# Query denominators summed four chunks at a time in eight partitions, in a graph layer fused with linear attention and a gated feed-forward

## The chip, the cores and the metric

The kernel runs on one core of a Trainium2 chip. The metric is device time in microseconds (us), the median of several executions. Beside the median stands one profiled execution, from which all rows below are read; its span runs from the first to the last instruction of the engines.

## The reference

`x` has 1250 rows (nodes) of 1024 columns, in float32. The layer normalises it, adds a graph convolution over 41,250 edges and a linear attention with 16 heads, and adds a gated feed-forward of a second normalisation. What matters here is the attention:

```python
phiQ = elu_plus_one(Q);  phiK = elu_plus_one(K)          # (1, 16, 1250, 64) each
S = jnp.einsum('bhki,bhkj->bhij', phiK, V)
Z = phiK.sum(axis=-2)                                     # one vector of 64 per head
num = jnp.einsum('bhqi,bhij->bhqj', phiQ, S)
denom = jnp.einsum('bhqi,bhi->bhq', phiQ, Z)[..., None] + EPS
context = num / denom
```

The kernel divides `phiQ` by the denominator before the product with `S`. A denominator is one number per head and node, so 16 x 1250 numbers in all.

## The kernel before, in words

Activations lie transposed, features in partitions. Every large product is made of three single-pass products of float32r parts: a value is split into a high part (a copy with rounding, by ScalarE) and a low part (the difference, by VectorE or GpSimd), and high x high, low x high and high x low are summed in PSUM. Weights stream from DRAM in slices of 128 x 512 into a ring of 10 slots, split there by ScalarE (`hi`, line 753) and GpSimd (`weight_lo`, line 443). A slot is free for its next slice when TensorE has used it for the last time, so each slab of weights follows TensorE closely at the switch from one slab to the next.

The stages in order are: keys and values (40 units), queries (24 units, lines 1552 to 1554), the graph's `h` units (20, lines 1431 to 1433), aggregation, mixing with `Wo`, and the feed-forward. The change lies in the query stage and the first `h` units. The queries are 8 blocks of 128 features (two heads each) times 3 chunks of nodes (418, 416, 416). I call the 24 units product 0 to 23, in the order in which TensorE makes them; each has 24 matmuls. Before, the chunk runs fastest. Each engine has its own program in order, joined by semaphores:

- TensorE: product i, then the denominator of i-2 (`denominator`, line 1568). The two slabs switch between products 11 and 12; after product 23 come the `h` units, the first of which has denominator 22 behind it and the second denominator 23.
- VectorE, for each i: `q_min` (line 1196, PSUM to `qmin`), `den_invert(i-3)` (line 1212, the reciprocal), `q_add` (line 1206, writes `phiq`), `den_apply(i-3)` (line 1219, `phiq` times the reciprocal).
- ScalarE, for each i: the exponential (line 832), the relu (line 835, which frees the PSUM bank), `den_copy(i-2)` (line 820, PSUM plus epsilon to `rec`). At i = 11 and 23 it makes six `hi` copies of the next slab before the exponential and two behind it.
- SyncE: `phin_store` (line 472) puts the divided `phiq` into DRAM (`phin_d`), one block of 1250 columns at a time, from three buffers.

Three PSUM banks serve all units in turn. The denominator before is one float32 product per unit: the stationary operand `zblk` is 128 x 128, with the sums of `phik` over the nodes copied along 64 columns for each head, so that each of the 128 partitions gets its head's denominator already in place.

Of the kernel before, what the change touches and what calls it, by code (L numbers as in the profile page):

```python
# [58 lines left out]
PHI_BUFS = 3  # L59
# [50 lines left out]

def units():

    u = [("kv", s, t) for s in range(4) for t in range(NT)]
    u += [("q", 0, 0), ("z", 0), ("z", 1)]
    u += [("q", f, c) for f in range(KD) for c in range(3) if f or c]
# [48 lines left out]
def build(nc, x, src_rows, dst_rows, wslices, wo, bkv, bq, gb, bo, scales, w3s, out):  # L164
    with ExitStack() as ctx:
# [53 lines left out]
        with ExitStack() as r2:  # L219
            hs = sb("hs", [P, 2, NT, 512], F32R, r2)  # L220
# [24 lines left out]
        with ExitStack() as r3:  # L245
            zblk = sb("zblk", [P, KD, P], F32, r3)
            qmin = sb("qmin", [P, 2, 418], F32, r3)
            qrel = sb("qrel", [P, 2, 418], F32, r3)
            rec = sb("rec", [P, 2, 418], F32, r3)
            phiq = sb("phiq", [P, PHI_BUFS, N], F32, r3)  # L250
# [14 lines left out]

        phin_d = nc.dram_tensor("phin_d", [KD, P, N], F32, kind="Internal").ap()
# [55 lines left out]
        den_done = sem("den_done")  # L322
# [130 lines left out]
        def _(sp):  # L453
# [16 lines left out]
            def phin_store(f):  # L470
                sp.wait_ge(phin_ready, 3 * (f + 1))
                sp.dma_start(phin_d[f], phiq[:, f % PHI_BUFS, :]).then_inc(phin_stored[f % PHI_BUFS], 16)
# [18 lines left out]
            for step in range(64):  # L491
# [7 lines left out]
                if step >= 40 and (step - 40) % 3 == 2 and (step - 40) // 3 >= 1:  # L499
                    phin_store((step - 40) // 3 - 1)  # L500
            phin_store(KD - 1)

            for b in range(PHI_BUFS):
                sp.wait_ge(phin_stored[b], 16 * len(range(b, KD, PHI_BUFS)))
# [113 lines left out]
        def _(pool):  # L618
# [65 lines left out]
            for b in range(PHI_BUFS):  # L684
                pool.wait_ge(phin_stored[b], 16 * len(range(b, KD, PHI_BUFS)))
# [21 lines left out]
        def _(act):  # L707
# [93 lines left out]
            def sums_out():  # L801
# [4 lines left out]
                for i in range(2):  # L806
                    u = UNIT["z", i]
                    wait_full(act, u)
                    act.wait_ge(z_cleared, 1)
                    z_ps = PS[:, bank(u), :].rearrange("p (a b) -> p a b", a=4)  # L810
                    nc.scalar.activation(zblk[0:64, 4 * i:4 * i + 4, 0:64], z_ps[0:64, :, 0:64], ACT.Copy)
                    nc.scalar.activation(zblk[64:P, 4 * i:4 * i + 4, 64:P], z_ps[64:P, :, 64:P],
                                         ACT.Copy).then_inc(acc_free[bank(u)], 1)

            def den_copy(i):
                n = CHUNKS[i % 3][1]
                act.wait_ge(den_done, i + 1)
                if i >= 2:
                    act.wait_ge(phin_ready, i - 1)
                nc.scalar.activation(rec[:, i % 2, 0:n], PS[:, 3 + i % 2, 0:n], ACT.Identity,  # L820
                                     bias=eps_sb).then_inc(den_read, 1)

            act.wait_ge(small_in, 32)
            for i in range(24):
                f, c = divmod(i, 3)
# [13 lines left out]
                if i >= 2:  # L839
                    den_copy(i - 2)  # L840
# [15 lines left out]

            act.wait_ge(deg_copied, 1)
# [4 lines left out]
            for t in range(NT):  # L862
# [4 lines left out]
                if t < 2:  # L867
                    den_copy(22 + t)
# [81 lines left out]
        def _(dve):  # L950
# [237 lines left out]
            dve.memset(zblk[:], 0.0).then_inc(z_cleared, 1)  # L1188
            dve.wait_ge(small_in, 32)

            def q_min(i):
                f, c = divmod(i, 3)
# [6 lines left out]
            def q_add(i):  # L1199
                f, c = divmod(i, 3)  # L1200
# [3 lines left out]
                if f >= PHI_BUFS and c == 0:  # L1204
                    dve.wait_ge(phin_stored[f % PHI_BUFS], 16 * (f // PHI_BUFS))
                dve.tensor_tensor(phiq[:, f % PHI_BUFS, o:o + n], qmin[:, i % 2, 0:n], qrel[:, i % 2, 0:n],
                                  ALU.add).then_inc(phiq_ready, 1)

            def den_invert(i):
                n = CHUNKS[i % 3][1]  # L1210
# [11 lines left out]
            for i in range(24):  # L1222
# [4 lines left out]
                if i >= 3:  # L1227
                    den_apply(i - 3)
# [504 lines left out]
```

## Time and profile before

| | us |
|---|---|
| median of 3 executions (lowest, highest) | 996.22 (995.83, 997.37) |
| the profiled execution | 995.84 |
| its span | 994.1 |
| TensorE busy in the span | 975.2 |
| VectorE, ScalarE, GpSimd busy | 543.9, 293.6, 142.4 |

The profiled execution is 0.4 us under the median and 1.7 us longer than its own span. TensorE is busy for 98% of the span at a granted clock of 0.999. A matmul's shown duration overlaps the next one's; what one costs is the distance from its start to the next start.

### The profile page before, as it was taken

To read this page: it belongs to the slowest core of one execution; us is meant where nothing else is said; L and a number is where in the kernel's file an instruction comes from. 1 tells how busy PE (TensorE), PEld (TensorE's weight loads), DVE (VectorE), ACT (ScalarE), POOL (GpSimd) and SP (SyncE) were. 2 spreads that over 40 slices of the span, in tenths; PEclk is the share of its full clock that TensorE was granted. 3 is DMA by queue.
4 is the path that set the end of the run, shared out by engine and by line. 5 is a ranking of instruction groups with operands and counts; after the bars stand their busy time and mean duration, and the time that the engine had idled before them with its cause. 6 is when DMAs were issued, how large, how long until landed. Compare 5 with 4: busy or idle time off the path is not lost.

```text
span 994.1 us, 13325 instructions
## 1 busy us (share of the span) xinstructions
PE 975.2 (98%) x4860; PEld 824.4 (83%) x4860; DVE 543.9 (55%) x1067; ACT 293.6 (30%) x585; POOL 142.4 (14%) x191
## 2 busy tenths in 40 slices
PE   5999999999999999999999999999999999999998
PEld 4887888888889989978786788767788999999986
DVE  6886578777763888782113556447557212122354
ACT  6873122232133343341213221114113312135300
POOL 7101001001011050050300000000201103064100
PEclk9999999999999999999999999999999999999999
DMA  7412013113021022122201465535422302010053
GB/s 269 150 49 86 5 30 117 28 31 100 16 77 36 26 90 73 52 69 95 96 12 55 147 204 172 157 119 186 170 80 90 123 1 85 1 43 1 22 190 139
DMA packets 46979, 86.78 MB, mean 87 GB/s; under 512 B 19036, under 2 KB 23388, under 8 KB 46896
## 3 DMA queue, kind: packets, MB, share of 16 engines
q1 hardware_dynamic: 38416, 57.28, 17.5%
q0 software_dynamic: 8480, 28.45, 8.7%
q8 instruction: 45, 0.74, 0.3%
q14 instruction: 38, 0.31, 0.1%
HBM read 61.62 MB, written 24.09 MB: 86 GB/s over the span
## 4 chain that ended last, share of the span: by engine, by line
PE 92%; DVE 3%; DMA 2%; ACT 1%; issue 1%; POOL 1%; SPq 0%; DVEq 0%; ACTq 0%; POOLq 0%
PE PS L1431 11%; PE PS L1433 11%; PE PS L1432 11%; PE PS L1552 9%; PE PS L1553 9%; PE PS L1554 9%; PE PS L1610 5%; PE PS L1612 4%; PE PS L1630 3%; PE PS L1631 3%; PE PS L1629 3%; PE PS L1471 2%; PE PS L1446 2%; PE PS L1683 2%; PE PS L1682 2%; PE PS L1681 2%
## 5 line engine op out<-in xcount | busy, mean ns | idle before, releaser
L1431 PE MATMUL PS<-ring,act_t 128*128 128x512 f32 (+1 forms) x480 | 194.7, 406 | 1.3 <-POOL ring L443 0.6
L1433 PE MATMUL PS<-ring,act_t 128*128 128x512 f32 (+1 forms) x480 | 190.7, 397 | 0.0
L1432 PE MATMUL PS<-ring,act_t 128*128 128x512 f32 (+1 forms) x480 | 190.3, 396 | 0.0
L1552 PE MATMUL PS<-act_t,ring 128*128 128x416 f32 (+1 forms) x432 | 159.3, 369 | 1.4 <-POOL ring L443 1.3
L1553 PE MATMUL PS<-act_t,ring 128*128 128x416 f32 (+1 forms) x432 | 152.2, 352 | 0.0
L1554 PE MATMUL PS<-act_t,ring 128*128 128x416 f32 (+1 forms) x432 | 151.7, 351 | 0.0
L1431 PEld LDWEIGHTS PS<-ring,act_t 128*128 128x128 f32 (+1 forms) x480 | 89.8, 187 | 23.9 <-POOL ring L443 1.6
L1433 PEld LDWEIGHTS PS<-ring,act_t 128*128 128x128 f32 (+1 forms) x480 | 89.5, 186 | 22.4
L1432 PEld LDWEIGHTS PS<-ring,act_t 128*128 128x128 f32 (+1 forms) x480 | 89.9, 187 | 21.2 <-issue 0.5
L1552 PEld LDWEIGHTS PS<-act_t,ring 128*128 128x128 f32 x432 | 81.3, 188 | 6.8 <-issue 3.4
L1553 PEld LDWEIGHTS PS<-act_t,ring 128*128 128x128 f32 x432 | 81.4, 188 | 4.0 <-issue 3.4
L1554 PEld LDWEIGHTS PS<-act_t,ring 128*128 128x128 f32 x432 | 81.2, 188 | 0.9
L1212 DVE RECIPROCAL rec<-rec 128x416 f32<-128x416 f32 (+1 forms) x24 | 65.9, 2747 | 0.0
L747 ACT ACTIVATE ctile<-PS 128x130 uint16<-128x130 f32 x100 | 23.7, 283 | 122.8 <-PE PS L1471 122.8
L627 POOL DMA_DIRECT2D stage_x<-in_wslices_dram x54 | 29.1, 544 | 198.2 <-DVE ring L443 194.4
L1362 DVE SCALAR_TENSOR_TENSOR hb<-PS,scl,sil 128x416 f32<-128x416 f32 (+1 forms) x12 | 7.8, 651 | 75.4 <-PE PS L1554 75.4
L627 POOL DMA_DIRECT2D stage<-in_wslices_dram x42 | 23.0, 550 | 173.2 <-DVE ring L443 170.6
L1147 DVE TENSOR_TENSOR kb<-PS,kvb 128x256 f32<-128x256 f32 (+1 forms) x40 | 16.9, 423 | 56.4 <-issue 31.1
L443 POOL TENSOR_TENSOR ring<-stage,ring 128x512 fp32r<-128x512 f32 x23 | 31.0, 1349 | 101.4 <-ACT ring L753 99.6
L443 POOL TENSOR_TENSOR ring<-stage_x,ring 128x512 fp32r<-128x512 f32 x28 | 38.3, 1367 | 30.1 <-ACT ring L753 27.0
L1077 DVE TENSOR_TENSOR oh_dst<-iota,kcur 128x520 bf16<-128x520 int16 x100 | 42.1, 421 | 0.0
L1076 DVE TENSOR_TENSOR oh_src<-iota,kcur 128x512 bf16<-128x512 int16 x100 | 41.8, 418 | 0.3
(195 smaller groups left out, 1650.7 us busy)
## 6 DMA issues: line engine op xcount, KB each, us to landing
stage_x<-in_wslices_dram POOLq DMA_DIRECT2D x54, 256.0 KB, 4.2
stage<-in_wslices_dram POOLq DMA_DIRECT2D x42, 256.0 KB, 3.7
xr<-x_d SPq DMA_DIRECT2D x18, 512.0 KB, 3.6
phin_d<-phiq SPq DMA_DIRECT2D x8, 625.0 KB, 3.1
xrow<-in_x_dram SPq DMA_DIRECT2D x9, 512.0 KB, 3.6
xh<-in_x_dram SPq DMA_DIRECT2D x18, 256.0 KB
x_d<-xh SPq DMA_DIRECT2D x18, 256.0 KB
x_d<-xr SPq DMA_DIRECT2D x9, 512.0 KB, 3.0
```

The lines of the kernel that those rows point to most:

```text
L443: eng.tensor_tensor(ring[:, slot(k), 1, :], stage_buf(n), ring[:, slot(k), 0, :].bitcast(F32), ALU.subtract).then_inc(w_ready, 1)
L627: pool.dma_start(stage_buf(n), wslices[n]).then_inc(stage_in[stage_slot(n)], 16)
L1076: dve.tensor_tensor(oh_src[:, b], count(P), pairs(kcur[:, dt % 2, j, 0], P), ALU.is_equal)
L1077: dve.tensor_tensor(oh_dst[:, b], count(WCOLS), pairs(kcur[:, dt % 2, j, 1], WCOLS), ALU.is_equal).then_inc(onehot, 1)
L1212: dve.reciprocal(rec[:, i % 2, 0:n], rec[:, i % 2, 0:n]).then_inc(rec_ready, 1)
L1431: pe.matmul(out_ap, node_rows(0, k, t), ring[:, slot(k0 + k), 0, :], start=(k == 0), stop=False)
L1432: pe.matmul(out_ap, node_rows(1, k, t), ring[:, slot(k0 + k), 0, :], start=False, stop=False)
L1433: ins = pe.matmul(out_ap, node_rows(0, k, t), ring[:, slot(k0 + k), 1, :], start=False, stop=(k == KD - 1))
L1552: pe.matmul(out_ap, w[0], x_t[:, 0, k, o:o + n], start=(k == 0), stop=False)
L1553: pe.matmul(out_ap, w[0], x_t[:, 1, k, o:o + n], start=False, stop=False)
L1554: ins = pe.matmul(out_ap, w[1], x_t[:, 0, k, o:o + n], start=False, stop=(k == nk - 1))
L1610: pe.matmul(out_ap, lhs, h_rows(half, 0, st), start=(st == 0), stop=False)
```

## The change

The query products run in another order (four feature blocks for one chunk of nodes, then the next chunk). The denominator of a unit becomes three single-pass products of parts (`z_hl`, `phi_hl`) with eight stationary columns, and four units sum into the same eight partitions: a group is four products, and row 2j+h holds head h of its block j. There are six groups. One reciprocal on 8 partitions serves a group. SyncE then stores the eight rows to DRAM (`rec_d`) and loads them back into 128 partitions (`rec_all`), each row to 64 partitions, in two DMAs. `phiq` is kept in nine buffers of one chunk, and `den_apply` runs eight products behind instead of three. ScalarE makes the high part of `phiq` (`phi_split`), VectorE the low part (`phi_rest`).

```diff
+PHI_BUFS = 9
+PHI_LAG = 8
+def q_chunk(i):
+    s, r = divmod(i, 12)
+    return 4 * s + r % 4, r // 4
...
+            rec_all = sb("rec_all", [P, 4, 418], F32, r3)
+            phiq = sb("phiq", [P, PHI_BUFS, 418], F32, r3)
...
+        rec_d = nc.dram_tensor("rec_d", [6, 4, 2, 418], F32, kind="Internal").ap()
...  SyncE
+            def phin_store(i):
+                f, c = q_chunk(i)
+                o, n = CHUNKS[c]
+                sp.wait_ge(phin_ready, i + 1)
+                sp.dma_start(phin_d[f, :, o:o + n], phiq[:, i % PHI_BUFS, 0:n]).then_inc(phin_stored[i % PHI_BUFS], 16)
+            def rec_spread(g):
+                n = CHUNKS[g % 3][1]
+                sp.wait_ge(rec_ready, g + 1)
+                sp.dma_start(rec_d[g].rearrange("a b n -> (a b) n")[:, 0:n], rec[0:8, 0:n]).then_inc(rec_stored, 16)
+                sp.wait_ge(rec_stored, 16 * (g + 1))
+                sp.wait_ge(phin_ready, 4 * g)
+                for h in range(2):
+                    sp.dma_start(rec_all[64 * h:64 * h + 64, :, 0:n],
+                                 rec_d[g, :, h, 0:n].unsqueeze(0).to_broadcast([64, 4, n])).then_inc(rec_in, 16)
...
-                if step >= 40 and (step - 40) % 3 == 2 and (step - 40) // 3 >= 1:
-                    phin_store((step - 40) // 3 - 1)
-            phin_store(KD - 1)
+            for i in range(24 + PHI_LAG):
+                if i >= PHI_LAG:
+                    phin_store(i - PHI_LAG)
+                if 7 <= i < 28 and i % 4 == 3:
+                    rec_spread((i - 7) // 4)
...  ScalarE
+            def phi_split(i):
+                n = CHUNKS[q_chunk(i)[1]][1]
+                act.wait_ge(phiq_ready, i + 1)
+                if i >= 2:
+                    act.wait_ge(phi_used, i - 1)
+                nc.scalar.activation(phi_hl[:, 0, i % 2, 0:n], phiq[:, i % PHI_BUFS, 0:n], ACT.Copy).then_inc(phi_hi, 1)
...
-                if i >= 2:
-                    den_copy(i - 2)
+                if i >= 1:
+                    phi_split(i - 1)
+                if i >= 5 and i % 4 == 1:
+                    den_copy((i - 5) // 4)
...  VectorE
+            def den_apply(i):
+                n = CHUNKS[q_chunk(i)[1]][1]
+                dve.wait_ge(rec_in, 32 * (i // 4 + 1))
+                dve.tensor_tensor(phiq[:, i % PHI_BUFS, 0:n], phiq[:, i % PHI_BUFS, 0:n], rec_all[:, i % 4, 0:n],
                                   ALU.mult).then_inc(phin_ready, 1)
             for i in range(24):
                 q_min(i)
-                if i >= 3:
-                    den_invert(i - 3)
+                if i >= 1:
+                    phi_rest(i - 1)
+                if i >= 6 and i % 4 == 2:
+                    den_invert((i - 6) // 4)
+                if i >= PHI_LAG:
+                    den_apply(i - PHI_LAG)
                 q_add(i)
-                if i >= 3:
-                    den_apply(i - 3)
...  in the first h units
-                if t < 3:
-                    den_invert(21 + t)
-                    den_apply(21 + t)
+                if t == 2:
+                    den_invert(5)
+                if t < PHI_LAG:
+                    den_apply(24 - PHI_LAG + t)
...  TensorE
-                for i in range(2):
-                    u = UNIT["z", i]
-                    b = open_unit(u)
-                    for j in range(4):
-                        ins = pe.matmul(PS[:, b, P * j:P * (j + 1)], ksum[:, P * (4 * i + j):P * (4 * i + j + 1)], ones[:],
-                                        start=True, stop=True)
-                    ins.then_inc(acc_full, 1)
+                u = UNIT["z", 0]
+                b = open_unit(u)
+                for f in range(KD):
+                    ins = pe.matmul(PS[:, b, f:f + 1], ksum[:, P * f:P * (f + 1)], ones[:, 0:1], start=True, stop=True)
+                ins.then_inc(acc_full, 1)
...
-                pe.matmul(PS[:, 3 + i % 2, 0:n], zblk[:, f, :], phiq[:, f % PHI_BUFS, o:o + n],
-                          start=True, stop=True).then_inc(den_done, 1)
+                pe.wait_ge(phi_lo, i + 1)
+                if j == 0 and g >= 2:
+                    pe.wait_ge(den_read, g - 1)
+                for z, b in ((0, 0), (0, 1), (1, 0)):
+                    ins = pe.matmul(PS[0:8, 3 + g % 2, 0:n], z_hl[:, z, i // 12, 8 * j:8 * j + 8], phi_hl[:, b, i % 2, 0:n],
+                                    start=(j == 0 and z + b == 0), stop=(j == 3 and z == 1))
+                ins.then_inc(phi_used, 1)
```

On VectorE in the middle of the query stage (line numbers of the changed file from here on: 1236 is `q_min`, 1261 `phi_rest`, 1267 the reciprocal, 1272 `den_apply`, 1246 `q_add`), one product before:

```order
L1196 TENSOR_SCALAR qmin<-PS,bq_sb 128x418 [waits acc_full]
L1212 RECIPROCAL rec<-rec 128x418 [waits den_read]
L1206 TENSOR_TENSOR phiq<-qmin,qrel 128x418 [waits phin_stored2,acc_free0,qact_ready]
L1219 TENSOR_TENSOR phiq<-phiq,rec 128x418 [waits phiq_ready,rec_ready]
```

and the rows of products 14 and 15 now:

```order
L1236 TENSOR_SCALAR qmin<-PS,bq_sb 128x418 [waits acc_full]
L1261 TENSOR_TENSOR phi_hl<-phiq,phi_hl 128x418 [waits phi_hi]
L1267 RECIPROCAL rec<-rec 8x416 [waits den_read]
L1272 TENSOR_TENSOR phiq<-phiq,rec_all 128x416 [waits rec_in]
L1246 TENSOR_TENSOR phiq<-qmin,qrel 128x418 [waits phin_stored5,acc_free1,qact_ready]
L1236 TENSOR_SCALAR qmin<-PS,bq_sb 128x418 [waits acc_full]
L1261 TENSOR_TENSOR phi_hl<-phiq,phi_hl 128x418 [waits phi_hi]
L1272 TENSOR_TENSOR phiq<-phiq,rec_all 128x416 [waits rec_in]
L1246 TENSOR_TENSOR phiq<-qmin,qrel 128x418 [waits phin_stored6,acc_free2,qact_ready]
```

The reciprocal stands in one product of four, and `den_apply`, which now waits for the loads into `rec_all`, has moved ahead of `q_add`.

On SyncE for the whole query stage, before:

```order
L472 DMA phin_d<-phiq 128x1250 [waits phin_ready] x8
```

and now for one group of four:

```order
L491 DMA phin_d<-phiq 128x418 [waits phin_ready] x4
L496 DMA rec_d<-rec 8x416 [waits rec_ready]
L500 DMA rec_all<-rec_d 64x4x416 [waits phin_ready,rec_stored]
L500 DMA rec_all<-rec_d 64x4x416
```

The store of a group's eight rows stands behind the fourth `phin_store` of the four before, and the two loads behind that store.

On TensorE at the start of the query stage, between product 0 and product 1, before:

```order
L1455 MATMUL PS<-ksum,kvb 128x128
L1539 MATMUL PS<-ones,ksum 128x128 [waits acc_free2,ksum_ready,consts]
L1539 MATMUL PS<-ones,ksum 128x128 x3
L1539 MATMUL PS<-ones,ksum 128x128 [waits acc_free0]
L1539 MATMUL PS<-ones,ksum 128x128 x3
L1552 MATMUL PS<-act_t,ring 128x416 [waits acc_free1]
```

and now, with the first denominator behind product 2 in the last two rows:

```order
L1514 MATMUL PS<-ksum,kvb 128x128
L1597 MATMUL PS<-ones,ksum 128x1 [waits acc_free2,ksum_ready,consts]
L1597 MATMUL PS<-ones,ksum 128x1 x7
L1609 MATMUL PS<-act_t,ring 128x418 [waits acc_free0]
...
L1625 MATMUL PS<-phi_hl,z_hl 8x418 [waits phi_lo,st_ready,acc_free2]
L1625 MATMUL PS<-phi_hl,z_hl 8x418 x2
```

The eight sums of keys have one output column each instead of 128, and a denominator is three matmuls that wait for the low part of `phiq` (`phi_lo`) instead of for `phiq` itself.

## Rows read from the trace of the kernel before

**Rows 1.** The page: busy us of each engine, share of the span, instructions.
```profile
PE 975.2 (98%) x4860; PEld 824.4 (83%) x4860; DVE 543.9 (55%) x1067; ACT 293.6 (30%) x585; POOL 142.4 (14%) x191
```

**Rows 2.** Timeline, TensorE, around one denominator: start us, us, line, out<-in.
```profile
349.14 0.86 PE L1568 MATMUL PS<-phiq,zblk 128*128 128x416 f32 x2
...
354.23 0.35 PE L1554 MATMUL PS<-act_t,ring 128*128 128x416 f32 x1
354.41 0.86 PE L1568 MATMUL PS<-phiq,zblk 128*128 128x416 f32 x2
...
355.30 0.35 PE L1553 MATMUL PS<-act_t,ring 128*128 128x416 f32 x1
```

**Rows 3.** Timeline, TensorE, one-column products and the sums of keys.
```profile
295.77 0.25 PE L1489 MATMUL PS<-ones,csum 128*98 128x1 f32 x2
295.89 0.44 PE L1552 MATMUL PS<-act_t,ring 128*128 128x418 f32 x1
...
301.43 1.95 PE L1539 MATMUL PS<-ones,ksum 128*128 128x128 f32 x16
303.13 0.43 PE L1552 MATMUL PS<-act_t,ring 128*128 128x416 f32 x1
```

**Rows 4.** Timeline, VectorE and ScalarE, one undisturbed product of the query stage.
```profile
349.34 0.65 DVE L1196 TENSOR_SCALAR qmin<-PS,bq_sb 128x418 f32<-128x418 f32 x1 [1.01 <-PE PS L1554]
349.91 2.76 DVE L1212 RECIPROCAL rec<-rec 128x418 f32<-128x418 f32 x1
350.03 0.55 ACT L832 ACTIVATE qmin<-qmin 128x418 f32<-128x418 f32 x1 [3.72 <-DVE qmin L1196]
350.49 0.59 ACT L835 ACTIVATE qrel<-PS,bq_sb 128x418 f32<-128x418 f32 x1
350.98 0.60 ACT L820 ACTIVATE rec<-PS,cmx 128x416 f32<-128x416 f32 x1
352.58 0.53 DVE L1206 TENSOR_TENSOR phiq<-qmin,qrel 128x418 f32<-128x418 f32 x1
353.03 0.58 DVE L1219 TENSOR_TENSOR phiq<-phiq,rec 128x418 f32<-128x418 f32 x1
```

**Rows 5.** Timeline, the switch of slabs at products 11 and 12.
```profile
357.84 1.36 DVE L1206 TENSOR_TENSOR phiq<-qmin,qrel 128x416 f32<-128x416 f32 x1
359.12 1.67 DVE L1219 TENSOR_TENSOR phiq<-phiq,rec 128x416 f32<-128x416 f32 x1
360.49 5.91 POOL L443 TENSOR_TENSOR ring<-stage_x,ring 128x512 fp32r<-128x512 f32 x4
...
367.13 0.86 PE L1568 MATMUL PS<-phiq,zblk 128*128 128x416 f32 x2
```

**Rows 6.** DMA issues of the whole run: KB each, median us from issue to landing.
```profile
xr<-x_d SPq DMA_DIRECT2D x18, 512.0 KB, 3.6
...
ct_d<-ctile SPq DMA_DIRECT2D x10, 320.0 KB, 2.2
kraw<-keys_d SPq DMA_DIRECT2D x100, 4.0 KB, 1.6
gb_sb<-in_gb_dram SPq DMA_DIRECT2D x1, 512.0 KB, 4.3
```

**Rows 7.** DMA issues between 136 and 144 us: a row spread over 128 partitions.
```profile
kvb<-in_bkv_dram SPq DMA_DIRECT2D x1, 256.0 KB, 3.6
```

**Rows 8.** Timeline, the last `phin_store`, its waiters, and the output of `h` unit 8.
```profile
450.12 0.32 SPq L472 DMA_DIRECT2D phin_d<-phiq  x1
453.28 0.34 SPq L540 DMA_DIRECT2D gb_sb<-in_gb_dram  x1
453.76 1.09 POOL L682 DMA_DIRECT2D ctu<-ct_d  x2 [17.17 <-DMA phin_d<-phiq]
478.85 0.69 ACT L848 ACTIVATE hs<-PS,dinv 128x512 fp32r<-128x512 f32 x1 [4.89 <-PE PS L1433]
480.31 2.74 POOL L443 TENSOR_TENSOR ring<-stage_x,ring 128x512 fp32r<-128x512 f32 x2 [25.47 <-ACT ring L753]
```

More of the change, by code:

```diff
@@ L108, in rows @@
     return min(P, N - t * P)
+def q_chunk(i):
+    s, r = divmod(i, 12)
+    return 4 * s + r % 4, r // 4
 def units():
     u = [("kv", s, t) for s in range(4) for t in range(NT)]
-    u += [("q", 0, 0), ("z", 0), ("z", 1)]
-    u += [("q", f, c) for f in range(KD) for c in range(3) if f or c]
+    u += [("q", 0, 0), ("z", 0)]
+    u += [("q", *q_chunk(i)) for i in range(1, 24)]
     u += [("h", 0, t) for t in range(NT)]
@@ L219, in build @@
         with ExitStack() as r2:
+            sb("pad3", [P, 2 * NT * 512 - 4 * 418], F32, r2)
+            phi_hl = sb("phi_hl", [P, 2, 2, 418], F32R, r2)
+        with ExitStack() as r2:
             hs = sb("hs", [P, 2, NT, 512], F32R, r2)
@@ L855, in cf_out @@
                 nc.scalar.activation(cf[:, t % 2], ctu[:, t % 2], ACT.Copy).then_inc(cf_ready, 1)
+            phi_split(23)
             act.wait_ge(deg_copied, 1)
@@ L1207, in q_add, with z_rest @@
                                   ALU.add).then_inc(phiq_ready, 1)
-            def den_invert(i):
-                n = CHUNKS[i % 3][1]
-                dve.wait_ge(den_read, i + 1)
-                dve.reciprocal(rec[:, i % 2, 0:n], rec[:, i % 2, 0:n]).then_inc(rec_ready, 1)
-            def den_apply(i):
-                f, c = divmod(i, 3)
-                o, n = CHUNKS[c]
-                dve.wait_ge(rec_ready, i + 1)
-                dve.wait_ge(phiq_ready, i + 1)
-                dve.tensor_tensor(phiq[:, f % PHI_BUFS, o:o + n], phiq[:, f % PHI_BUFS, o:o + n], rec[:, i % 2, 0:n],
+            def z_rest():
+                u = UNIT["z", 0]
+                dve.wait_ge(z_hi, 1)
+                for g in range(2):
+                    o = slice(64 * g, 64 * g + 64)
+                    z_out = dve.tensor_tensor(z_hl[o, 1, :, g:g + 31:10], PS[o, bank(u), 0:KD].rearrange("p (a b) -> p a b", a=2),
+                                              z_hl[o, 0, :, g:g + 31:10].bitcast(F32), ALU.subtract)
+                z_out.then_inc(acc_free[bank(u)], 1)
@@ new lines, in phi_rest, with den_invert @@
+            def phi_rest(i):
+                n = CHUNKS[q_chunk(i)[1]][1]
+                dve.wait_ge(phi_hi, i + 1)
+                dve.tensor_tensor(phi_hl[:, 1, i % 2, 0:n], phiq[:, i % PHI_BUFS, 0:n],
+                                  phi_hl[:, 0, i % 2, 0:n].bitcast(F32), ALU.subtract).then_inc(phi_lo, 1)
+            def den_invert(g):
+                n = CHUNKS[g % 3][1]
+                dve.wait_ge(den_read, g + 1)
+                dve.reciprocal(rec[0:8, 0:n], rec[0:8, 0:n]).then_inc(rec_ready, 1)
@@ L1234, in _ @@
                     dve.tensor_copy(deg[0:last, 0, NT - 1:NT], PS[0:last, 7, NT - 1:NT]).then_inc(deg_copied, 1)
+            phi_rest(23)
             dve.wait_ge(root_deg, 1)
```

83 lines of the change are left out of this document (41 added, 42 removed).

## The prediction, made before the changed kernel was run

> **What bounds the kernel now.** I read the page first: TensorE is busy for 975.2 us, 98% of the span, and the next engine, VectorE, for 543.9 [rows 1]. Then I read the timeline of the query stage, TensorE alone. There one product of 24 matmuls follows the next with no idle, each with its denominator behind it: from one denominator's start to the next are 354.41 - 349.14 = 5.27 us [rows 2]. So anything taken off TensorE's queue counts in full and work moved to another engine is free, but only while those engines deliver before TensorE comes to the product that needs them. I then followed VectorE, ScalarE and SyncE through one product, since the change lengthens the way from a query product to its denominator and puts a trip through DRAM into VectorE's order.
>
> **TensorE's own work.** The matmul ahead of a denominator starts at 354.23 and the second one behind it at 355.30 [rows 2]. That is 1.07 us, of which two ordinary steps of 0.19 (24 of them and a denominator make the 5.27) are not the denominator's: it costs 0.69. Now three single-pass products over the same 416 or 418 columns take 3 x 0.19 = 0.57. Their stationary operand has 8 columns instead of 128, which no row shows; I take the step as unchanged, since the moving columns are the same. The saving is 24 x 0.125 = 3.0 us, and the product's period becomes 5.15.
>
> The 8 sums of keys are 16 passes of 128 columns, 303.13 - 301.43 = 1.70 us; two passes of one column take 295.89 - 295.77 = 0.12, so 16 take about 0.96 [rows 3]. That saves 0.7 us.
>
> At the switch from slab to slab TensorE waits for GpSimd's low parts: the last ended at 366.40, and product 12 was over at 367.13, 12.7 us after product 10, where two undisturbed periods are 10.5 [rows 5]. That chain starts from the end of product 10 through `q_min`, not from TensorE's later work, so what the two denominators inside it save is waited away. Two switches with two denominators each give back 4 x 0.125 = 0.5.
>
> **Work beside it.** VectorE loses 18 of 24 reciprocals of 2.7 us and gains 24 differences of about 0.58; ScalarE changes 24 copies of 0.60 for 24 of 0.55 and 6 of 0.60 [rows 4]. All of this lies beside TensorE; its cover is the 5.15 us of each product, and it is worth nothing by itself.
>
> The last `phin_store` moves from 450.12 to behind `h` unit 7. ScalarE's output of unit 8 starts at 478.85, and a unit takes 4.89 + 0.69 = 5.58, so that of unit 7 starts at 473.3, and VectorE's two steps of 0.7 behind it last until 475.4. GpSimd waits for all of them before it loads `ctu` and makes the low parts of the last six slices. The store lands in less than the 3.16 us of the row (450.12 to 453.28), then 1.09 for the two loads: free at about 479.4, while its next work comes at 480.31 [rows 8]. With 0.9 us of cover I cost it at nothing; if that is used up, the low parts for the second half of the `h` units are late by the excess, and TensorE waits for at most that.
>
> **The trip through DRAM.** This is the term that decides. I lay out a group in the middle of the stage, with 0 at the end of product 14, in steps of [rows 4] and [rows 2]. VectorE's `q_min` starts 0.20 later (349.34 against 349.14) and ends at 0.85; ScalarE's exponential starts at 0.89, relu at 1.35, and `phi_split` in the old copy's place from 1.84 to 2.39. `phi_rest` is done at 3.0, the group's reciprocal at 5.6, `den_apply` and `q_add` at 6.55. Product 15 ended at 5.15, so its `q_min` is late: 6.55 to 7.2, `phi_split` until 8.74, `phi_rest` until 9.36, `den_apply(7)` until A = 9.9.
>
> Only now can SyncE go on, since the next group's store of eight rows is queued behind `phin_store(7)`. That issue takes 0.32 [rows 8]. The store follows, behind 209 KB in the same queue: 320 KB land in 2.2 and 4 KB in 1.6 [rows 6], so I take 1.7. Then two loads of 64 partitions x 4 x 416 floats, 836 KB in all. The trace shows none like it. From below: 4 KB land in 1.6 us and 512 KB in 3.6 [rows 6], so 836 KB take 1.6 + 2.0 x 836/512 = 4.9. From above: 256 KB spread from one row to 128 partitions take 3.6 [rows 7], so 1.6 + 2.0 x 836/256 = 8.1, though that load shared the queues with a store; I use 7.8. `gb_sb`, 512 KB spread from one row, took 4.3 [rows 6]: 1.6 + 2.7 x 836/512 = 6.0. It is the nearest in size and kind, and I take 6.0. The data are there at 9.9 + 0.35 + 1.7 + 0.05 + 6.0 = 18.0.
>
> Who waits: `den_apply(8)` stands ahead of `q_add(16)` in VectorE's order, and behind that stand `q_min(17)`, ScalarE's exponential, relu and `phi_split(16)`, and `phi_rest(16)`, without which denominator 16 can't start. From the landing these are 0.07 + 0.5 + 0.45 + 0.65 + 0.04 + 0.46 + 0.49 + 0.55 + 0.04 + 0.58 + 0.07 = 3.9 us. So denominator 16 can start at 21.9, and TensorE has finished product 18 at 4 x 5.15 = 20.6. TensorE waits 1.3 us. After such a wait VectorE is still behind, and comes to the next A 0.5 to 0.6 later, which makes 1.9 in the repeated case. Denominators 16 and 20 pay that. Denominator 12 pays about 2.0: at the switch two SBUF operations of VectorE under GpSimd's took 2.95 us instead of 1.1 (357.84 to 360.79) [rows 5], so A comes at 12.6 to 13.4 after product 10, the landing 8.1 later, the denominator 3.9 after that (24.6 to 25.4), and TensorE is there at 12.7 + 0.57 + 4.58 + 0.57 + 4.58 = 23.0. Group 0 has no earlier `den_apply` to wait for, and groups 4 and 5 fall into the `h` units, where two units of 5.6 us cover them. Last, at the second switch VectorE is some 1.6 us late, GpSimd's low parts start later by that, and about 0.5 is left on TensorE.
>
> The sum: -3.0 - 0.7 + 0.5 + 2.0 + 1.9 + 1.9 + 0.5 = +3.1 us. The profiled execution of 995.84 becomes 998.9; its median stood 0.4 higher, so I predict 999.3.
>
> Each load reaches only 64 partitions. A rule on this comes from the Trainium skill's "SBUF — State Buffer", section "Door 1: The DMA port swizzle": partitions 0 to 63 lie behind 8 of the 16 ports, measured at 196 GB/s where 128 partitions got 328; and "DMA: Bandwidth & Descriptors" says in its table of advice that transfers to disjoint halves serialize. No row here shows a transfer to 64 partitions. By its asymptote of 218 GB/s the two would take an estimated 3.9 us plus the 2.0 fixed, so 5.9 together. By that the sum would be 0.3 us below mine, and the landing of 4.9 would be out.
>
> **The rivals.** (1) The trip is hidden: store and loads land early enough that no denominator waits. For it speaks that the slack is missed by only 1.3 us, in a chain of a dozen steps; against it that the 836 KB would have to land in about 4.1 us, when 512 KB alone took 3.6. The side changes at a landing of 5.0 us, where the three waits just equal what TensorE saves. Then only the first three terms stay: -3.2, 993.0.
> (2) The loads run at the rate of an ordinary load, 4.9 us. Each of the three waits shrinks by 1.1 to a sum of 2.5 and the late switch goes: -0.7, 995.5, no measurable change.
> (3) The two halves follow each other at half the rate, or a spread is as slow as [rows 7]: 7.8 us. Each wait grows by 1.8: +3.1 + 5.4 = +8.5, 1004.7. For it speaks the one row of a spread of 2 KB pieces; against it `gb_sb`, which took 4.3 where that rate gives 5.6.
> (4) The eight-column products are not at 0.19 each. At 0.27 (the step behind a change of operand, which [rows 3] show between 295.89 and the next at about 296.16) they cost 0.81 each instead of 0.69: +2.9 instead of -3.0, 998.9 with all else hidden.
>
> **How the numbers follow.** Forecast (997.3 to 1001.5) 0.45; rival 1 0.21, rival 2 0.15, rival 3 0.15, rival 4 0.04. Within 0.2% is 994.2 to 998.2, about what a measurement can't tell from no change. Slower takes most of the forecast (0.40), and rivals 3 and 4: 0.59. Faster takes rival 1: 0.21. The same takes rival 2 and the forecast's lower edge: 0.20. The range from 992.8 to 1004.8 leaves out half of rival 3 and a part of rival 1.
>
> **What would show it.** VectorE idle ahead of `den_apply` at products 12, 16 and 20, some 4 to 5 us each, released by the DMA into `rec_all`; TensorE idle ahead of denominators 12, 16 and 20, released by `phi_rest`, about 2 us each. `rec_all` landing near 5.6 us behind its issue. Three products of a denominator spaced by 0.19, and the product's period 5.15 where nothing waits. GpSimd's wait for the stores over before 480. The forecast is wrong if TensorE is busy through the stage (rival 1 or 2), or if a denominator's three products take over 0.7 us.

## The result: 1.2% slower

The median went from 996.72 us (6 runs, 995.36 to 997.59) to 1007.84 us (6 runs, 1006.58 to 1011.96). The ratio is 1.0117, with a 95% interval of 1.0097 to 1.0137. The profiled execution of the changed kernel took 1006.92 us with a span of 1004.9; it stands 11.1 above that of before. 999.3 was predicted, with a range up to 1004.8: the sign was right, the size was not.

The page of the changed kernel, which answers to [rows 1]:

```profile
PE 976.8 (97%) x4884; PEld 822.0 (82%) x4884; DVE 510.8 (51%) x1075; ACT 295.6 (29%) x589; POOL 148.9 (15%) x191
```

TensorE is busy 1.6 us longer and the span is 10.8 longer, so most of the loss is idle TensorE. GpSimd is busy 6.5 us longer with the same 191 instructions. That second number is the clue that the prediction had no term for.

The best view for the rest is a list of the starts of the denominators on TensorE's timeline. Before, 24 of them run from 312.29 to 438.86, which is 126.57 us; now they run from 312.47 to 450.05, which is 137.58. The difference of 11.0 holds the whole change of the profiled execution (behind the last denominator the changed kernel is 0.4 shorter, ahead of the first 0.2 longer). I call the distance from the start of denominator k to that of k+1 step k. One after the other, the differences are:

| steps | before, us | after, us | difference |
|---|---|---|---|
| 15 with nothing else in them | 5.25 to 5.27 | 5.10 to 5.14 | -2.1 |
| 9 and 21, the switches of slabs | 7.47, 7.60 | 10.60, 9.78 | +5.3 |
| 10 and 20 | 5.24, 5.26 | 6.68, 6.59 | +2.8 |
| 13, 15, 19 | 5.26 to 5.27 | 5.57, 7.86, 7.58 | +5.2 |
| 22 | 6.27 | 6.13 | -0.1 |

**The products themselves.** The row that answers to [rows 2], and the sums of keys of [rows 3] (timeline of TensorE):

```profile
301.56 1.84 PE L1597 MATMUL PS<-ones,ksum 128*128 128x1 f32 x16
303.26 0.44 PE L1609 MATMUL PS<-act_t,ring 128*128 128x418 f32 x1
...
312.47 0.73 PE L1625 MATMUL PS<-phi_hl,z_hl 128*8 128x418 f32 x3
313.03 0.35 PE L1609 MATMUL PS<-act_t,ring 128*128 128x418 f32 x1
```

Three products of a denominator take 313.03 - 312.47 = 0.56 us. The sums of keys still take 303.26 - 301.56 = 1.70, although each pass has one column instead of 128.

**The first switch,** which answers to [rows 5] (timelines of VectorE, GpSimd and TensorE; the last number in brackets is the idle time just before):

```profile
355.81 0.59 DVE L1261 TENSOR_TENSOR phi_hl<-phiq,phi_hl 128x416 fp32r<-128x416 f32 x1 [1.55 <-ACT phi_hl L858]
356.32 2.73 DVE L1267 RECIPROCAL rec<-rec 8x416 f32<-8x416 f32 x1
356.39 4.25 POOL L460 TENSOR_TENSOR ring<-stage,ring 128x512 fp32r<-128x512 f32 x1 [46.66 <-ACT ring L784]
358.99 0.52 DVE L1272 TENSOR_TENSOR phiq<-phiq,rec_all 128x418 f32<-128x418 f32 x1
359.43 1.66 DVE L1246 TENSOR_TENSOR phiq<-qmin,qrel 128x416 f32<-128x416 f32 x1
...
362.37 6.03 POOL L460 TENSOR_TENSOR ring<-stage_x,ring 128x512 fp32r<-128x512 f32 x4
368.45 0.45 PE L1609 MATMUL PS<-act_t,ring 128*128 128x418 f32 x1 [0.74 <-POOL ring L460]
369.13 1.03 PE L1625 MATMUL PS<-phi_hl,z_hl 128*8 128x416 f32 x3
```

In the kernel before, the same first low part took 1.30 us:

```profile
357.45 1.30 POOL L443 TENSOR_TENSOR ring<-stage,ring 128x512 fp32r<-128x512 f32 x1 [47.91 <-ACT ring L753]
```

Now it starts 0.07 us behind VectorE's reciprocal and takes 4.25, which is 2.95 longer. The reciprocal ends at 359.05 and the low part at 360.64. I call this the lock: GpSimd's operation is under way in the trace, but behaves as if it could not work until VectorE's reciprocal is over. `den_apply`, right behind the reciprocal, takes an undisturbed 0.52; `q_add`, the next, takes 1.66. GpSimd's last low part comes at 368.40 instead of 366.40, although the slab's end had come 1.1 us earlier (denominator 9 at 358.53, before at 359.66). The second switch shows the same: 4.27 us from 430.99.

**The clock.** Windows behind the switch (length, busy us of PE, PEld, DVE, ACT, POOL, granted clock, DMA share, GB/s):

```profile
366.00:370.00 4.00, 2.51 (x11) 1.61 (x11) 1.92 (x2) 0.00 (x0) 3.84 (x5) 0.92 0.32 102
370.00:374.00 4.00, 4.00 (x16) 3.85 (x15) 2.02 (x1) 1.49 (x3) 3.69 (x7) 0.65 0.96 241
374.00:378.00 4.00, 4.00 (x23) 3.65 (x22) 1.66 (x3) 0.98 (x3) 1.84 (x2) 1.00 1.04 374
```

TensorE was never idle in 370 to 374 and yet issued 16 products where the next window has 23: the granted clock was 0.65, so part of the time at the lower level, 1.2 GHz. Before it TensorE had waited. Step 10 was 1.4 us longer for that than in the kernel before, and 1.6 longer than an undisturbed step of 5.12. Behind the wait of denominator 20 the same is seen (426 to 432, in windows of two us: 0.85, 0.50, 0.80), and step 20 was 1.3 longer than before, 1.5 longer than an undisturbed one. Behind the 2.58 us of denominator 16 the clock stayed at 1.00. In the kernel before it is 1.00 in the four us behind its switch. These windows come from one profiled execution of each kernel. The mean granted clock of the whole program shows the others: 0.994 to 0.997 in the six executions of the changed kernel, and 0.996 to 1.000 in 17 of the kernel before, 13 of them at 0.999 or 1.000.

**The trip through DRAM,** group 2 (SyncE, VectorE and TensorE):

```profile
392.39 0.34 SPq L496 DMA_DIRECT2D rec_d<-rec  x1
394.05 1.24 SPq L500 DMA_DIRECT2D rec_all<-rec_d  x2
400.58 0.59 DVE L1272 TENSOR_TENSOR phiq<-phiq,rec_all 128x416 f32<-128x416 f32 x1 [5.37 <-DMA rec_all<-rec_d]
404.64 0.72 PE L1625 MATMUL PS<-phi_hl,z_hl 128*8 128x416 f32 x3 [2.58 <-DVE phi_hl L1261]
```

From the store's issue to that of the loads are 1.66 us, from the first load's issue to its use 400.5 - 394.05 = 6.45, and from the landing to denominator 16 another 4.1. Group 3 repeats it: 5.36 us of waiting on VectorE, 2.32 on TensorE. Denominator 12 did not wait, and denominator 14 waited 0.3.

### The profile page after: what moved, and what is told of

Read it like the earlier page. It is cut to its first block, busy times and chain, and to the rows that moved or that the text cites. A ratio compares the mean times of both kernels' runs of the same rounds, so it can differ in the third digit from the quotient of the medians.

```text
span 1004.9 us, 13391 instructions
## 1 busy us (share of the span) xinstructions
PE 976.8 (97%) x4884; PEld 822.0 (82%) x4884; DVE 510.8 (51%) x1075; ACT 295.6 (29%) x589; POOL 148.9 (15%) x191
## 4 chain that ended last, share of the span: by engine, by line
PE 86%; DVE 4%; DMA 4%; ACT 2%; issue 1%; POOL 1%; SPq 0%; DVEq 0%; POOLq 0%; ACTq 0%
PE PS L1490 11%; PE PS L1492 11%; PE PS L1491 11%; PE PS L1609 7%; PE PS L1610 7%; PE PS L1611 7%; PE PS L1668 5%; PE PS L1670 4%; PE PS L1688 3%; PE PS L1689 3%; PE PS L1687 3%; PE PS L1530 2%; PE PS L1505 2%; DMA rec_all<-rec_d 2%; PE PS L1741 2%; PE PS L1740 2%
## 5 line engine op out<-in xcount | busy, mean ns | idle before, releaser
L460 POOL TENSOR_TENSOR ring<-stage,ring 128x512 fp32r<-128x512 f32 x23 | 37.0, 1608 | 106.4 <-ACT ring L784 104.6
L869 ACT ACTIVATE qmin<-qmin 128x416 f32<-128x416 f32 (+1 forms) x24 | 13.3, 554 | 91.5 <-DVE qmin L1236 91.5
L1668 PE MATMUL PS<-hs,cf 128*128 128x512 f32 (+1 forms) x100 | 39.3, 393 | 0.3 <-issue 0.3
```

Of the source, the lines that this page charges most:

```text
L460: eng.tensor_tensor(ring[:, slot(k), 1, :], stage_buf(n), ring[:, slot(k), 0, :].bitcast(F32), ALU.subtract).then_inc(w_ready, 1)
L1668: pe.matmul(out_ap, lhs, h_rows(half, 0, st), start=(st == 0), stop=False)
```

## The experiments

In each I give the length from denominator 0 to denominator 23 (before 126.57, after 137.58), which takes the scatter of the rest of the program out. It is read from one profiled execution of each kernel. Runs of before beside the first four new kernels had a median of 996.07, beside the next four 996.43, beside the last two 996.73.

**Is it the place of the reciprocal?** The first question was why GpSimd was kept out. Either VectorE's reciprocal and the low part are bad neighbours wherever they meet, or it is the form with 8 partitions. The first new kernel moves the reciprocal, the second changes its partitions.

```diff
+                if i % 12 == 10:
+                    den_invert((i - 6) // 4)
...
-                if i >= 6 and i % 4 == 2:
+                if i >= 6 and i % 4 == 2 and i % 12 != 10:
```

> The group reciprocal stands ahead of phi_rest instead of behind it, but only in products 10 and 22, the two that meet GpSimd's low parts of the next slab. Theory A: GpSimd's first low part took 4.25 us (start 356.39) because VectorE went into the reciprocal directly behind phi_rest, an operation with two SBUF inputs, and kept GpSimd out until the reciprocal was over at 359.05. Then here the first low part takes 1.3 to 1.5 us at both switches, product 12 and the first h unit lose about 3 us of waiting each, and the low clock behind product 12 goes with it: 1007.8 - 6 - 1.4 = about 1000.4. Theory B: the reciprocal on 8 partitions keeps GpSimd out wherever it stands (the one on 128 did not). Then the low part, which starts some 0.5 us before the reciprocal ends, takes about 1.8 us; the time is within 1 us of A's, so the duration decides. Theory C: the low parts were slow for another reason (three differences of VectorE instead of two): 4.25 us stay and the time stays at 1007.8.

Measured: 1006.04 us (ratio 1.0093, 1.0076 to 1.0110); length 136.12. With the reciprocal ahead of `phi_rest`, it has almost ended when GpSimd comes, and the low part takes 2.63:

```profile
355.82 2.73 DVE L1267 RECIPROCAL rec<-rec 8x416 f32<-8x416 f32 x1
358.03 2.63 POOL L460 TENSOR_TENSOR ring<-stage,ring 128x512 fp32r<-128x512 f32 x1 [46.80 <-ACT ring L784]
```

The reciprocal ended at 358.55. If it holds GpSimd to its end in both kernels, 0.5 us of the 2.63 are its share, and the rest is that of VectorE's two-input operations behind it, as in [rows 5]. This run does not settle the question: 2.63 us fits neither the 1.3 to 1.5 of theory A nor the 1.8 of theory B, and only C's 4.25 is out. The time fell much less than the expected 7: step 9 is 1.1 us shorter than in the changed kernel and step 10 is 1.2 shorter, but steps 11 to 15 take 2.2 us more together.

```diff
+            dve.memset(rec[:], 1.0)
...
-                dve.reciprocal(rec[0:8, 0:n], rec[0:8, 0:n]).then_inc(rec_ready, 1)
+                dve.reciprocal(rec[:, 0:n], rec[:, 0:n]).then_inc(rec_ready, 1)
```

> The changed kernel with the reciprocal on all 128 partitions of rec (the 120 others hold ones or old values that nothing reads), in the same place behind phi_rest. Theory A (held from the two-input operation through the next): GpSimd's first low part at the switch takes 4.25 us again. Theory B (8 partitions matter): 1.3 to 1.5 us as before, and about 3 us less at each switch.

Measured: 1008.72 us (one run); length 138.78. The time did not move, but the lock was gone, in the same place of VectorE's order. That is theory B, and A is out:

```profile
356.62 2.75 DVE L1268 RECIPROCAL rec<-rec 128x416 f32<-128x416 f32 x1
356.69 1.30 POOL L460 TENSOR_TENSOR ring<-stage,ring 128x512 fp32r<-128x512 f32 x1 [46.97 <-ACT ring L784]
```

Step 9 fell from 10.60 to 7.80 and step 21 from 9.78 to 8.11. The reciprocal is as long as with 8 partitions (2.73), so nothing was saved by using few of them. What was won came back at once: denominator 12 waited, and step 11 was 13.12 us. The kernel with one buffer, below, shows why.

**How many partitions does it take?** The reciprocal of group 1 on 32 partitions and that of group 4 on 64, the others on 8:

```diff
+            dve.memset(rec[:], 1.0)
...
-                dve.reciprocal(rec[0:8, 0:n], rec[0:8, 0:n]).then_inc(rec_ready, 1)
+                parts = {1: 32, 4: 64}.get(g, 8)
+                dve.reciprocal(rec[0:parts, 0:n], rec[0:parts, 0:n]).then_inc(rec_ready, 1)
```

> The changed kernel with the reciprocal on 32 partitions in product 10 and on 64 in product 22, on 8 elsewhere. The 8-partition reciprocal kept GpSimd out at both switches (first low part 4.25 us), the 128-partition one at neither (1.30). If the line lies at 32 or below, both first low parts take 1.3 us; if it lies between 32 and 64, 4.25 and 1.3; if anything under 128 keeps GpSimd out, 4.25 twice.

Measured: 1008.43 us (one run); length 139.46.

```profile
356.25 2.73 DVE L1269 RECIPROCAL rec<-rec 32x416 f32<-32x416 f32 x1
356.31 1.69 POOL L460 TENSOR_TENSOR ring<-stage,ring 128x512 fp32r<-128x512 f32 x1 [46.90 <-ACT ring L784]
...
435.30 2.74 DVE L1269 RECIPROCAL rec<-rec 64x416 f32<-64x416 f32 x1
435.36 1.69 POOL L460 TENSOR_TENSOR ring<-stage,ring 128x512 fp32r<-128x512 f32 x1 [61.82 <-ACT ring L784]
```

None of the three outcomes that I had written down came: there is a middle level. In this place 8 partitions keep GpSimd out, 32 and 64 cost it 0.4 us, 128 nothing. The 32 and the 64 were each seen once. Where between 8 and 32 the change lies was not tried.

**The trip alone, with a second buffer.** `rec_b` beside `rec_all`, so that the loads need not wait for the last `den_apply` of the group before and can start one product earlier:

```diff
-                sp.wait_ge(phin_ready, 4 * g)
...
+                if g >= 2:
+                    sp.wait_ge(phin_ready, 4 * (g - 1))
...
-                    sp.dma_start(rec_all[64 * h:64 * h + 64, :, 0:n],
+                    sp.dma_start((rec_all if g % 2 else rec_b)[64 * h:64 * h + 64, :, 0:n],
...
+                if 6 <= i < 27 and i % 4 == 2:
+                    rec_spread((i - 6) // 4)
...
-                if 7 <= i < 28 and i % 4 == 3:
-                    rec_spread((i - 7) // 4)
...
-                dve.tensor_tensor(phiq[:, i % PHI_BUFS, 0:n], phiq[:, i % PHI_BUFS, 0:n], rec_all[:, i % 4, 0:n],
+                dve.tensor_tensor(phiq[:, i % PHI_BUFS, 0:n], phiq[:, i % PHI_BUFS, 0:n], (rec_all if i // 4 % 2 else rec_b)[:, i % 4, 0:n],
```

> rec_all has two buffers, and SyncE stores and loads a group right behind its reciprocal, ahead of the phin_store of that product, so the trip no longer starts from den_apply of the group before. Everything else as changed. If the trip in that order is what denominators 14, 16 and 20 waited for (0.3, 2.7 and 2.5 us with the lost gain), these waits go, VectorE waits less than 1 us for rec_all, and the low clock behind denominator 20 (6.6 us for a product of 5.12) goes too: 1007.8 - 5.5 - 1.4 = about 1001. The rival is that the landing itself is too slow for a lag of eight products: then VectorE still waits for rec_all by more than 3 us a group and the time falls by under 2 us.

Measured: 1007.73 us (ratio 1.0120, 1.0103 to 1.0137); length 136.11. The wait for `rec_all` fell from 5.4 to 0.3 us, and another took its place. SyncE now issued a `phin_store` behind the loads, and `q_add`, which reuses its buffer, waited for it. The expected 1001 us missed this second wait:

```profile
393.23 0.60 DVE L1255 TENSOR_TENSOR phiq<-qmin,qrel 128x418 f32<-128x418 f32 x1 [4.46 <-DMA phin_d<-phiq]
...
396.69 1.20 PE L1634 MATMUL PS<-phi_hl,z_hl 128*8 128x418 f32 x3 [2.21 <-DVE phi_hl L1270]
```

TensorE waited 2.2 and 2.6 us, at denominators 15 and 19 instead of 16 and 20.

This kernel has another use. Its first switch is as long as that of the changed kernel (10.45 against 10.60), yet the clock stayed up behind it and step 10 took 5.12. It fell later, behind the wait of denominator 15 (396 to 400: 0.61, 0.53):

```profile
358.00:368.00 10.00, 6.31 (x27) 3.88 (x25) 6.30 (x7) 3.14 (x7) 9.28 (x7) 1.00 0.53 129
368.00:370.00 2.00, 1.99 (x10) 1.66 (x11) 1.06 (x2) 0.42 (x1) 1.99 (x4) 1.00 0.32 98
```

**Both: reciprocal first, two buffers.** The kernel above, and in every group:

```diff
+                if i >= 6 and i % 4 == 2:
+                    den_invert((i - 6) // 4)
                 if i >= 1:
                     phi_rest(i - 1)
...
```

> The two buffers with the early trip, and the reciprocal ahead of phi_rest in every group. If both theories hold nothing is left of the 11 us but a switch like before's: 1007.8 - 6 (switches) - 5.5 (waits) - 2.9 (low clock) = 993.4, which would be 3.3 us under the kernel before, the 24 x 0.145 that the products save. If they overlap (one wait covers the other), 996 to 1000.

Measured: 998.58 us (ratio 1.0023, 1.0014 to 1.0033); length 128.00. That lies within the 996 to 1000 expected if one wait covers the other. No denominator but 15 (0.6) waits for more than 0.2 us in the middle of the stage; the switches are 9.34 and 8.98. VectorE still waits for a `phin_store` by 3.9 and 3.4 us, now inside TensorE's slack. The reciprocal on 8 partitions is still there. The two edits alone had brought 1.8 and 0.1 us of the median, together they brought 9.3 (the reciprocal was moved in two groups there and in all six here).

**One buffer, early GpSimd, early store.**

```diff
-                if i >= 1:
-                    phi_rest(i - 1)
                 if i >= 6 and i % 4 == 2:
                     den_invert((i - 6) // 4)
+                if i >= 1:
+                    phi_rest(i - 1)
...
+                if 6 <= i < 27 and i % 4 == 2:
+                    rec_store((i - 6) // 4)
...
-                dve.reciprocal(rec[0:8, 0:n], rec[0:8, 0:n]).then_inc(rec_ready, 1)
+                dve.reciprocal(rec[:, 0:n], rec[:, 0:n]).then_inc(rec_ready, 1)
```

> Three edits on the changed kernel: the reciprocal stands ahead of phi_rest and runs on 128 partitions, and SyncE stores the eight rows right behind the reciprocal while the two loads stay where they were, behind the fourth phin_store of the group before, with one buffer. From the end of den_apply the trip is then only the loads (0.35 + 0.05 + 6.45 = 6.9 us instead of 8.5), and it starts 1.4 us earlier: denominator 16 would be ready before TensorE comes. Expected: no wait above 0.3 us ahead of denominators 12 to 20, GpSimd's first low part 1.3 us at both switches, switches at 7.5 to 8.0 us between denominators 9 and 10; 996.1 - 19 x 0.145 + 0.5 = about 993.8. The rival: the loads of group 1 meet GpSimd's weight loads behind the switch (they landed in over 10 us when GpSimd was early), VectorE waits 3 to 5 us more there, and with the low clock it comes out at 997 to 999.

Measured: 1003.49 us (ratio 1.0070, 1.0050 to 1.0089); length 134.43. That is beyond both the expected 993.8 and the 997 to 999 of its rival, which named the cause but took it too small. The switches are down to 7.70 and 7.85 and no later denominator waits, but denominator 12 does, and behind it the clock is 0.50 from 380 to 390 us (step 12 takes 7.84):

```profile
365.33 1.29 POOL L663 DMA_DIRECT2D stage<-in_wslices_dram  x2
366.28 1.28 SPq L503 DMA_DIRECT2D rec_all<-rec_d  x2
366.61 2.16 POOL L663 DMA_DIRECT2D stage_x<-in_wslices_dram  x4
...
379.99 0.59 DVE L1278 TENSOR_TENSOR phiq<-phiq,rec_all 128x416 f32<-128x416 f32 x1 [9.44 <-DMA rec_all<-rec_d]
...
384.05 1.20 PE L1631 MATMUL PS<-phi_hl,z_hl 128*8 128x418 f32 x3 [7.51 <-DVE phi_hl L1267]
```

The loads of `rec_all` were issued among GpSimd's loads of weights, 256 KB each, 2 of them in the microsecond before and 4 beside it, and took 13.7 us from issue to use instead of 6.45. In the kernel with 128 partitions, the one with 32 and 64, and this one, all with GpSimd early at the first switch, VectorE waited 11.29, 10.97 and 9.44 us there. In the changed kernel GpSimd was late: SyncE issued these loads at 367.72, GpSimd its first at 368.34, and VectorE had the data at 375.33 after waiting 1.77, 7.6 us behind the issue. So the long landings go with weights issued ahead of these loads, in three kernels of three; no run moved the loads of weights alone.

**The kernel that both faults point to.** Reciprocal first and on 128 partitions, two buffers; SyncE's order is the store of the eight rows, a `phin_store`, then the loads, all at i%4 = 2:

```diff
+                if 6 <= i < 27 and i % 4 == 2:
+                    rec_store((i - 6) // 4)
...
+                if 6 <= i < 27 and i % 4 == 2:
+                    rec_spread((i - 6) // 4)
```

> As the one before, but with two buffers and the loads right behind the third phin_store, so they no longer wait for den_apply of the group before, while each phin_store is issued before the loads and not behind them. Expected: VectorE waits for neither rec_all nor a phin_store beyond 0.5 us, and group 1's loads are issued before GpSimd's weight loads; no denominator waits; about 993.6. The rival as above, but weaker: 995 to 997.

Measured: 995.01 us (11 runs, 993.02 to 1000.46; ratio 0.9984, 0.9968 to 0.9999), at the edge of what can be told from no change, and 1.4 above the expected 993.6; length 125.59. VectorE waits for no DMA in the stage. The trip of group 2 is

```profile
382.83 0.29 SPq L499 DMA_DIRECT2D rec_d<-rec  x1
383.77 0.32 SPq L494 DMA_DIRECT2D phin_d<-phiq  x1
384.23 1.24 SPq L510 DMA_DIRECT2D rec_b<-rec_d  x2
```

where the median landing of the loads into `rec_b` is 5.6, and its loads are issued 9.8 us earlier than in the changed kernel. Group 1's go out ahead of GpSimd's first load of weights at 366.69, and VectorE doesn't wait for them. The switches are 8.13 and 7.84. Step 10 is 6.24: in the profiled execution the clock fell here also.

```profile
366.00:368.00 2.00, 1.27 (x5) 0.96 (x5) 1.70 (x2) 0.00 (x0) 1.99 (x4) 0.73 0.35 65
368.00:370.00 2.00, 2.00 (x7) 1.51 (x6) 0.65 (x1) 1.15 (x3) 2.00 (x4) 0.50 0.90 251
```

**Half the bytes.** The loads bring two of the four chunks, and `den_apply` uses each twice; the output differs by that.

```diff
-                    sp.dma_start(rec_all[64 * h:64 * h + 64, :, 0:n],
+                    sp.dma_start(rec_all[64 * h:64 * h + 64, 0:2, 0:n],
...
-                dve.tensor_tensor(phiq[:, i % PHI_BUFS, 0:n], phiq[:, i % PHI_BUFS, 0:n], rec_all[:, i % 4, 0:n],
+                dve.tensor_tensor(phiq[:, i % PHI_BUFS, 0:n], phiq[:, i % PHI_BUFS, 0:n], rec_all[:, i % 2, 0:n],
```

> The changed kernel with each load of two chunks' rows instead of four (418 KB in two DMAs instead of 836); chunks 2 and 3 of a group are divided by the denominators of chunks 0 and 1, so the quotients of half the queries are not the reference's. If the bytes set the landing, the pair lands in about 4.3 us from its first issue instead of 6.45, denominators 14, 16 and 20 wait some 2 us less each (0.3, 2.7 and 2.5 us before), the low clock behind denominator 20 goes, and the time falls by 5 to 7 us to about 1002. If the fixed part sets it, the landing stays above 5.5 us and the time within 2 us of 1007.8.

Measured: 1002.25 us (ratio 1.0055, 1.0037 to 1.0072), as expected if the bytes set the landing; length 132.10. The page's rows of these loads, of the changed kernel and of this one (count, KB each, median us to landing):

```profile
rec_all<-rec_d SPq DMA_DIRECT2D x8, 416.0 KB, 5.7
```

```profile
rec_all<-rec_d SPq DMA_DIRECT2D x8, 208.0 KB, 3.7
```

2.0 us less of landing, and no denominator between the switches waits for it. VectorE still waits 2.95 for the data in group 2, inside the slack of TensorE. The switches stay long (11.16 and 11.20).

**No loads at all,** `rec_all` holding ones, with the reciprocal on 8 partitions and on 128:

```diff
-                sp.wait_ge(rec_stored, 16 * (g + 1))
-                sp.wait_ge(phin_ready, 4 * g)
-                for h in range(2):
-                    sp.dma_start(rec_all[64 * h:64 * h + 64, :, 0:n],
...
-                dve.wait_ge(rec_in, 32 * (i // 4 + 1))
```

> The changed kernel without the two loads and without den_apply's wait for them: rec_all holds ones, so phiq is not divided by its denominator. All other work stays, the store of eight rows too. The trip's whole price is the difference: waits ahead of denominators 14, 16 and 20 go (0.3, 2.6, 2.3 us), and the low clock behind denominator 20 (1.3); the two switches stay at about 10.5 and 9.8 us with GpSimd's first low part at 4.25. Expected 1007.8 - 6.5 = 1001.3. If the low clock behind product 12 is a matter of luck in where the waits fall, another 1.4 may come or go.

> The same with the reciprocal on 128 partitions: neither trip nor lock. What is left of the change is its gain on TensorE: 19 x 0.145 = 2.8 us less than before, with a switch of 7.5 to 8.1 us for denominators 9 to 10, thus 993.3 to 994. If something else of the change costs time, it comes out at 996 or above.

Measured: 1002.86 us (ratio 1.0060, 1.0044 to 1.0077), length 131.69, for 8 partitions; 994.62 us (ratio 0.9984, 0.9971 to 0.9997), length 123.73, for 128; 1001.3 and 993.3 to 994 were expected. Without the loads no denominator waits. The two differ in the reciprocal's partitions alone: 8.2 us of the median and 8.0 of the length, which are the steps 9 and 21 (11.15 and 10.79 against 7.55 and 7.67, 6.7 us) and step 10 (6.37 against 5.12, 1.3 us). The slowest of the ten executions with 128 partitions (997.87) lies below the fastest of the four with 8 (1000.78). GpSimd's first low part beside the reciprocal, 8 partitions and then 128:

```profile
357.71 4.25 POOL L460 TENSOR_TENSOR ring<-stage,ring 128x512 fp32r<-128x512 f32 x1 [46.79 <-ACT ring L780]
```

```profile
356.09 1.30 POOL L460 TENSOR_TENSOR ring<-stage,ring 128x512 fp32r<-128x512 f32 x1 [46.75 <-ACT ring L780]
```

The clock at 366 to 374 is 0.73, 0.50, 0.50 and 0.57 in two-us windows with 8, and 1.00 in each with 128. With 8 the dip begins inside step 9, which ends at 371.00. The profiled execution with 128 is one of the fastest of its ten (992.83, in a spread of 992.62 to 997.87), whose mean clocks run from 0.997 to 1.000, so not every execution need look like this trace.

## Why the prediction was too low

**Denominators, -3.0 predicted.** Right in size: -2.1 in the 15 undisturbed steps and -0.1 in step 22, with the rest inside the steps that waited. 3 x 0.19 = 0.57 was assumed and 0.56 measured; an ordinary step is 5.12 (5.15 predicted) where it had been 5.26. Rival 4 is out.

**Sums of keys, -0.7 predicted, nothing measured.** 16 passes took 1.70 before and now. I took the price of a one-column pass from a pair in [rows 3]. The change takes columns from the moving operand; the stationary one is loaded 16 times with 128 columns in both kernels (the loads are busy for 1.87 us in both). That these loads set the pace fits, but no run varied them.

**"All of this lies beside TensorE ... and it is worth nothing by itself."** This is the step that failed: the work moved to VectorE was put at nothing. It counted VectorE's reciprocals by how many there are and how long they last, both of which were right (2.73 us), and not by whom they keep out. The switches cost 5.3 us more, where the absorbed denominators and the late second switch were to cost 1.0. The last two kernels, which differ in nothing else, price it: 8.2 us for 8 partitions instead of 128, of which at least 1.3 came through the clock in the profiled executions. In [rows 5] I had read that VectorE's two-input operations slow down beside GpSimd, and laid that on VectorE's side only. The Trainium skill, "SBUF — State Buffer", section "SBUF: two separate sides", says that VectorE and GpSimd share a pair of ports as an exclusive lock, and that VectorE takes it in a fast two-port mode or with two inputs in SBUF. A reciprocal has one. By that rule GpSimd should not have been held by a reciprocal outside the two-port mode, and with 128 partitions it isn't (1.30); with 8 it is (4.25). Where they differ the measurement stands. Why so few partitions change it is open: no run shows which mode VectorE ran in.

**The trip, +5.8 predicted for denominators 12, 16 and 20; +5.2 measured, at 14, 16 and 20.** Sized nearly rightly. Landing 6.45 us where 6.0 was taken; VectorE idle 5.4; TensorE 2.6 and 2.3 where 1.9 were expected. That the sum came so near is in part luck: the waits at 16 and 20 were longer than forecast, and the 2.0 at denominator 12 did not come. There VectorE waited 1.77 us for the data and TensorE not at all, since, as I read it, TensorE had stood still for GpSimd in step 9 and run slowly in step 10, and given the loads that time. So the lock hid one of the three waits. The runs without loads confirm the other two in place (no waits) and the half loads show that they hang on the bytes. Rivals 1 to 3 are out; the rate of an ordinary load (4.9) and the slow one (7.8) lie on either side of what was seen. By the rule on 64 partitions of the Trainium skill's "SBUF — State Buffer", section "Door 1: The DMA port swizzle", the estimate was 5.9, which is 0.5 below the measured 6.45, and no run set the same bytes on 128 partitions against it.

**The clock, no term.** +2.8 us in steps 10 and 20. I had taken TensorE's idle time as the whole price of a wait. In this trace two waits were followed by a stretch with a low granted clock, and the step behind each was 1.3 to 1.4 us longer than in the kernel before. It isn't a fixed surcharge: the kernel with two buffers alone had as long a switch and no dip behind it, the one with both faults mended a shorter switch and a dip. Executions of one and the same kernel differ in it as well. What decides was not found.

**The sum.** Between the +3.1 predicted and the +11.1 of the profiled execution are 8.0 us: 4.3 for the switches, 2.8 for the clock, 0.9 ahead of the stage (-0.7 predicted, +0.2 measured), 0.7 for denominators whose saving lies inside the disturbed steps, -0.6 for the trip, -0.4 behind the stage, and 0.3 outside the span.

The change's own gain is small, and its intervals only just leave out no change: without loads and without the lock it was 2.1 us of the median (994.62 against 996.73; ratio 0.9984, 0.9971 to 0.9997), against the 2.8 expected. With its loads and the two faults mended it kept 1.4 (995.01 against 996.43).

## What to carry to other kernels

An operation moved beside the engine that bounds the kernel is free only if it leaves the third engine alone: look at that engine's rows next to the new form, here 8 partitions, which made the reciprocal no shorter (2.73 us against 2.75 with 128) and stopped GpSimd. Waits hide one another, so an edit that shows nothing by itself is not refuted until the wait beside it is gone: one alone moved the median by 1.8 or 0.1 us, both together by 9.3, though the pair also moved the reciprocal in four more groups. And when an engine comes free earlier, ask which transfers it starts: behind GpSimd's earlier loads of weights, 836 KB took 13.7 us from issue to use instead of 6.45.

## What the runs showed of the hardware

- A reciprocal of float32 on 8 partitions by 416 (2.73 us) that started 0.07 us ahead of a GpSimd operation stretched that operation from 1.30 us to 4.25. On 32 and on 64 partitions the operation took 1.69, on 128 it took 1.30.
- TensorE's granted clock fell to between 0.50 and 0.53 in two-us windows during or behind its waits, for 2 to 10 us, in the query stage of ten of the twelve kernels' profiled executions. Behind the first switch it fell in seven (switches of 7.80 to 11.16 us) and not in five (7.47, 7.55, 7.70, 8.10 and 10.45 us), so the length of the wait alone does not decide.
- Passes with one moving column cost as much as with 128 (0.106 us), 16 of them in a row with 128 stationary columns each.
